# Row sums with the residual's addition, squares on ScalarE, rows normalised a chunk later

## What is computed

```python
x = layernorm(x + attn(x))      # attn: time-mixed k, v, r; WKV scan; gate; product with Wo
x = layernorm(x + ffn(x))       # ffn: 8 experts, the 2 best per token, 256 -> 1024 -> 256

def layernorm(x, eps=1e-5):
    m = mean(x, -1); v = var(x, -1)
    return (x - m) / sqrt(v + eps)

# the scan, per channel d and batch b, over the 2048 tokens
no  = max(o, u + k);  y = (exp(o-no)*p + exp(u+k-no)*v) / (exp(o-no)*q + exp(u+k-no))
no2 = max(w + o, k);  p, q, o = exp(w+o-no2)*p + exp(k-no2)*v, exp(w+o-no2)*q + exp(k-no2), no2
attn = (sigmoid(r) * y) @ Wo.T
```

## Time and profile before

| | |
|---|---|
| median of 3 runs | 699.39 us (697.89 to 700.32) |
| the profiled execution's own time | 698.79 us |
| its span in the profile | 696.8 us |
| busy: PE, DVE, ACT, POOL | 630.9, 464.1, 377.9, 333.2 us |
| chain that ended last, by engine | PE 64%, DVE 16%, issue 8%, ACT 4%, DMA 3%, POOL 2% |
| DVE busy in slices 4 to 13 of 40 (52 to 226 us) | 9 or more tenths up to slice 12 |

### The profile page before, as it was taken

One profiled execution on the slowest core, in us unless ns is written; L12 is line 12 of the kernel. 1 busy time (PEld: TensorE's weight loads), 2 busy tenths in 40 slices (PEclk: granted clock), 3 DMA queues, 4 the chain that ended last, 5 costly groups with the idle time before them and its releaser, 6 DMA issues.

```text
span 696.8 us, 14651 instructions
## 1 busy us (share of the span) xinstructions
PE 630.9 (91%) x4525; PEld 581.3 (83%) x4525; DVE 464.1 (67%) x1075; ACT 377.9 (54%) x690; POOL 333.2 (48%) x322
## 2 busy tenths in 40 slices
PE   8999999999977788999999999999999999999800
PEld 5787887878854578999999999999999999999700
DVE  4879999999998566556556565565565465545334
ACT  3566686585764133645464646466464646464317
POOL 6111037536546768239356384356394275222325
PEclk9999999999989779999999999999999999999955
DMA  8500222321324745532534425325317313231376
GB/s 254 157 32 0 91 91 70 132 83 55 107 86 154 232 148 151 162 60 63 144 48 146 71 42 160 60 49 144 72 24 183 47 42 47 48 48 15 36 226 276
DMA packets 53309, 70.61 MB, mean 101 GB/s; under 512 B 5482, under 2 KB 46900, under 8 KB 53076
## 3 DMA queue, kind: packets, MB, share of 16 engines
q1 hardware_dynamic: 31012, 43.24, 18.8%
q0 software_dynamic: 13216, 17.09, 13.4%
q10 hardware_dynamic: 8976, 8.82, 4.5%
HBM read 40.86 MB, written 29.06 MB: 100 GB/s over the span
## 4 chain that ended last, share of the span: by engine, by line
PE 64%; DVE 16%; issue 8%; ACT 4%; DMA 3%; POOL 2%; SPq 0%; DVEq 0%; ACTq 0%; POOLq 0%
PE hT_ps L871 27%; PE y_ps L880 26%; PE vr_ps L708 3%; PE k_ps L708 2%; PE xT_ps L889 2%; ACT zz L1133 2%; DVE o_all L1221 2%; POOL records_dram L614 2%; DMA zz<-x_dram 1%; DVE newton L1244 1%; DVE newton L1249 1%; DVE stats L1319 1%; DVE newton L1242 1%; DMA recs<-records_dram 1%; DVE num L1311 1%
## 5 line engine op out<-in xcount | busy, mean ns | idle before, releaser
L871 PE MATMUL hT_ps<-xTh,wx 128*128 128x256 f32 x1120 | 207.5, 283 | 2.6 <-DVE aTl L1191 1.3
L652 POOL DMA_INDIRECT x_dram<-y_sb,dest x70 | 108.5, 1550 | 195.3 <-DVE y_sb L1208 128.1
L880 PE MATMUL y_ps<-wx,aTh 128*128 128x256 f32 x1088 | 191.1, 279 | 3.0 <-DVE y_sb L1208 3.0
L871 PEld LDWEIGHTS hT_ps<-xTh,wx 128*128 128x128 f32 x1120 | 174.8, 189 | 3.3 <-DVE aTl L1191 2.4
L1191 DVE TENSOR_TENSOR aTl<-hT_ps,aTh 128x512 fp32r<-128x512 f32 x140 | 93.3, 688 | 121.7 <-ACT aTh L1094 121.7
L880 PEld LDWEIGHTS y_ps<-wx,aTh 128*128 128x128 f32 x1088 | 165.5, 189 | 3.4 <-issue 3.4
L871 PE MATMUL hT_ps<-xTl,wx 128*128 128x256 f32 x560 | 156.9, 280 | 0.0
L880 PE MATMUL y_ps<-wx,aTl 128*128 128x256 f32 x544 | 151.7, 279 | 0.0
L1088 ACT ACT_TABLE_LOAD x33 | 42.3, 1283 | 162.5 <-PE hT_ps L871 160.8
L1088 ACT ACTIVATE hT_ps<-hT_ps,b_c 128x256 f32<-128x256 f32 x280 | 113.5, 468 | 22.8 <-PE hT_ps L871 21.2
L614 POOL DMA_INDIRECT records_dram<-rec,slot_i x64 | 76.7, 1198 | 67.6 <-DVE rec L1352 35.9
(11 more groups left out here) (203 smaller groups left out, 853.5 us busy)
## 6 DMA issues: line engine op xcount, KB each, us to landing
staging<-in_L_ffn_W SPq DMA_DIRECT2D x16, 1024.0 KB
recs<-records_dram ACTq DMA_DIRECT2D x33, 261.0 KB, 3.0
xin<-in_L_attn_x SPq DMA_DIRECT2D x16, 256.0 KB, 4.3
xres<-in_L_attn_x SPq DMA_DIRECT2D x16, 256.0 KB, 3.1
x_dram<-rec SPq DMA_DIRECT2D x16, 256.0 KB, 3.4
zz<-x_dram SPq DMA_DIRECT2D x8, 512.0 KB, 9.2
out<-zz SPq DMA_DIRECT2D x8, 512.0 KB, 3.5
records_dram<-pad_rec SPq DMA_DIRECT2D x8, 261.0 KB, 2.9
```

The costliest lines, as they stand in the source:

```text
L652: pool.indirect_dma_start(sums, bass.IndirectOffsetOnAxis(ap=dest[t.slot][:, h:h + 1], axis=0), y_sb[t.slot][:, h, :], None, bounds_check= ...
L871: ins = pe.matmul(hT_ps[b][:, f, :], wx[:, s, part, off:off + P], xpart[t.slot % 2][:, cc, :], start=k == 0, stop=k == len(terms) - 1)
L880: ins = pe.matmul(y_ps[h], apart[t.slot % 2][:, fc, h * P:(h + 1) * P], wx[:, s, part, off:off + C], start=k == 0, stop=k == len(terms) - 1)
```

## The change

DVE: each of the two residual additions per chunk becomes two instructions of 128 x 256 (one per tile) that also write the sum of the row into `sum_1`. `statistics` is gone (four bn_stats, four bn_aggr). ACT: a new stage `square_rows` of chunk i-1 stands where `normalise_x1` stood: one ACTIVATE makes -mean of the four tiles from `sum_1`, then four ACTIVATEs square (row - mean) and write the sums into `sum_2`; each of these waits for the one before. `normalise_x1` now runs in step i on chunk i-2, between `exponents` and `bonuses`. POOL: `spread_of` waits for the squares, and has three operations in place of four. `sum_1` is one buffer: the first residual addition of a chunk waits until -mean of the chunk before is made (`mean_done`).

```diff
@@ POOL @@
             def spread_of(c):
-                pool.wait_ge(mv_done, c.upto(J))
-                pool.tensor_tensor(var_e[:], mv[:, :, 1], eps_b[:], ALU.add).then_inc(vare_done, 1)
-                pool.tensor_scalar(neg_mean[:], mv[:, :, 0], -1.0, 0.0, ALU.mult, ALU.add).then_inc(vare_done, 1)
-                pool.wait_ge(vare_done, c.upto(3, 2))
+                pool.wait_ge(squared, c.upto(J))
+                pool.tensor_scalar(var_e[:], sum_2[:], 1.0 / C, EPS, ALU.mult, ALU.add).then_inc(vare_done, 1)
+                pool.wait_ge(vare_done, c.upto(2, 1))
@@ ACT @@
+            def square_rows(c):
+
+                act.wait_ge(res_done, c.upto(RES))
+                after(act, rstd_done, (c - 1).upto(1))
+                act.activation(neg_mean[:], sum_1[:], ACT.Copy, scale=-1.0 / C).then_inc(mean_done, 1)
+                act.wait_ge(mean_done, c.upto(1))
+                for j in range(J):
+                    after(act, squared, c.number * J + j)
+                    act.activation(squares[:], xres[c.slot][:, j // TH, j % TH, :], ACT.Square, bias=neg_mean[:, j:j + 1],
+                                   accum_out=sum_2[:, j:j + 1]).then_inc(squared, 1)
@@ ACT, step @@
+                if (i - 2).exists:
+                    normalise_x1(i - 2)
+                if i.exists:
                     bonuses(i)
...
                 if (i - 1).exists:
-                    normalise_x1(i - 1)
+                    square_rows(i - 1)
@@ DVE @@
-            def statistics(c):
-                dve.wait_ge(res_done, c.upto(2))
-                for j in range(J):
-                    dve.bn_stats(stats[:, j, :], xres[c.slot][:, j // TH, j % TH, :]).then_inc(bn_done, 1)
-                dve.wait_ge(bn_done, c.upto(J))
-                take_wait(dve)
-                for j in range(J):
-                    dve.bn_aggr(mv[:, j, :], stats[:, j, :]).then_inc(mv_done, 1)
@@ DVE, add_residual @@
-                dve.tensor_tensor(xres[c.slot][:, b], wo_bank(c, b), xres[c.slot][:, b], ALU.add).then_inc(res_done, 1)
+                    after(dve, mean_done, (c - 1).upto(1))
+                for h in range(TH):
+                    dve.scalar_tensor_tensor(out=xres[c.slot][:, b, h], in0=wo_bank(c, b)[:, h, :], scalar=1.0, in1=xres[c.slot][:, b, h],
+                                             op0=ALU.mult, op1=ALU.add,
+                                             accum_out=sum_1[:, b * TH + h:b * TH + h + 1]).then_inc(res_done, 1)
```

More of the change, by code:

```diff
@@ L186, in build @@
         neg_mean = sb("neg_mean", [P, J])
-        stats = sb("stats", [P, J, 6])
-        mv = sb("mv", [P, J, 2])
+        sum_1 = sb("sum_1", [P, J])
+        sum_2 = sb("sum_2", [P, J])
+        squares = sb("squares", [P, C])
         phase_a = ExitStack()
@@ L295, in build @@
         ln_done, r0_done, div_done, mixed_done = sem("ln_done"), sem("r0_done"), sem("div_done"), sem("mixed_done")
-        wo_done, res_done, bn_done, mv_done = sem("wo_done"), sem("res_done"), sem("bn_done"), sem("mv_done")
+        wo_done, res_done, mean_done, squared = sem("wo_done"), sem("res_done"), sem("mean_done"), sem("squared")
         vare_done, rstd_done, x1_done = sem("vare_done"), sem("rstd_done"), sem("x1_done")
@@ L320, in build @@
         c_bn, c_mv, c_var, c_rstd, c_res = (sem(n) for n in ("c_bn", "c_mv", "c_var", "c_rstd", "c_res"))
+        RES = B * TH
         REC_DMAS = 2 * J * 16
@@ L586, in spread_of @@
             def spread_of(c):
-                pool.wait_ge(mv_done, c.upto(J))
-                pool.tensor_tensor(var_e[:], mv[:, :, 1], eps_b[:], ALU.add).then_inc(vare_done, 1)
-                pool.tensor_scalar(neg_mean[:], mv[:, :, 0], -1.0, 0.0, ALU.mult, ALU.add).then_inc(vare_done, 1)
-                pool.wait_ge(vare_done, c.upto(3, 2))
+                pool.wait_ge(squared, c.upto(J))
+                pool.tensor_scalar(var_e[:], sum_2[:], 1.0 / C, EPS, ALU.mult, ALU.add).then_inc(vare_done, 1)
+                pool.wait_ge(vare_done, c.upto(2, 1))
                 pool.tensor_tensor(rstd[:, c.slot, :], var_e[:], half_neg[:], ALU.pow).then_inc(vare_done, 1)
-                pool.wait_ge(vare_done, c.upto(3))
+                pool.wait_ge(vare_done, c.upto(2))
                 pool.tensor_tensor(shift[:, c.slot, :], neg_mean[:], rstd[:, c.slot, :], ALU.mult).then_inc(rstd_done, 1)
@@ L765, in project_out @@
                         pe.wait_ge(gate_in, 48)
-                    after(pe, res_done, (c - 1).upto(2))
+                    after(pe, res_done, (c - 1).upto(RES))
                 elif c.number >= NCH - 2:
@@ L769, in project_out @@
                 else:
-                    pe.wait_ge(res_done, c.upto(2, 1))
+                    pe.wait_ge(res_done, c.upto(RES, TH))
                 pe.wait_ge(mixed_done, c.upto(B, n + 1))
@@ L783, in turn_early @@
                 if n == 0:
-                    pe.wait_ge(res_done, Step(None, NCH - 1, 2, NCH).upto(2))
+                    pe.wait_ge(res_done, Step(None, NCH - 1, 2, NCH).upto(RES))
                 else:
@@ L1377, in step @@
                     stages = [(stabilise, i)] + opening + [(divide, i - 1), (place, i - 3), (accumulate, i), (residual_0, i - 1), (numerator, i),
-                              (residual_1, i - 1), (statistics, i - 1), (choose, i - 2), (lower_halves, i + 2)]
+                              (residual_1, i - 1), (choose, i - 2), (lower_halves, i + 2)]
                     if i.number == NCH - 1:
@@ L1381, in step @@
                 elif i.number == NCH:
-                    stages = [(divide, i - 1), (residual_0, i - 1), (residual_1, i - 1), (statistics, i - 1), (choose, i - 2),
+                    stages = [(divide, i - 1), (residual_0, i - 1), (residual_1, i - 1), (choose, i - 2),
                               (place, i - 2)]
```

## The result

The changed kernel takes 704.72 us (median of 5 runs, 703.1 to 706.71) where the kernel before takes 699.39 (697.89 to 700.85): ratio 1.0069, 95% interval 1.0044 to 1.0095. It is slower by 0.7%, 5.3 us. The profiled execution took 704.72, span 702.9. Times within a kernel are those of its one profiled execution; for whole kernels the ratios count.

What follows compares the result with a forecast made beforehand. The prediction took DVE to bound the full steps, PE's chain a floor 1.05 us below. Terms +0.4 (step 2), -0.7, -0.9, +3.4, +0.4 sum to +2.6 us: 701.4 by the profiled execution, 702.0 as median, range 696.5 to 706.5.

Steps and rivals of the forecast that it cites:

- S = 3.0 us: ACT's `square_rows` per chunk: -mean 0.2 plus four squares with their sums at 0.70 each; ends 2.2 and 3.6.
- Rival 1: Sums nearly free on ACT: squares 2.2 us (deciding below 2.35), steps at PE's floor 25.15, end +1.8; 696.3 us; chance 0.17.
- DVE's additions, +0.25 per batch row: DVE's residual additions: two instructions for one add 0.19 us, the sum perhaps 0.1; 0.25 per batch row, 0.5 per chunk.
- Rival 4: DVE's additions with a sum run at half rate, 0.27 us more per 256 columns; 703.6 us; chance 0.05.
- ACT bounds the steps at 25.95, three times -0.25: Three full middle steps: ACT's loop of 22.93 plus the squares replaces DVE's 26.20 us; -0.7 in all.
- DVE's work per step falls to 24.85 us, below PE's floor: Full steps: DVE's 26.20 us lose 1.85 of statistics and gain 0.5 of additions; PE's floor is 25.15.
- My part on POOL: POOL: one of four tiny operations goes, `spread_of` takes 1.6 us and hides in a middle step.
- Step 6, -0.9 and a start of step 7 1.2 us earlier: Step 6: DVE's own work counts, -1.85 + 0.5, with 0.5 of waiting for scores; step 7 begins 1.2 us earlier.
- End of the phase, +3.4: Last chunks, cover gone: odds, squares, `spread_of`, rows in a chain; last rows transposed at 241.4 for 237.95, +3.4 us.
- PE's clock, +0.4: End of the phase: longer PE idle ahead of 224.5 may keep the clock low through idle products; half of 0.8 us.
- Rival 3: End of the phase: something else already holds the last rows, leaving only the steps' gain, -1.2; 698.2 us; chance 0.1.
- rival 2: Squares dear at 3.6 us (deciding above 3.25): ACT's loop 26.55 bounds every step, end +5.4; 706.5 us; chance 0.2.

Runs made afterwards that it cites:

- e_bufs: Changed kernel with four result buffers for the squares, so no square waits for the one before; ratio 1.0036 to the kernel before.
- e_order: Changed kernel with ACT squaring the rows ahead of the odds in steps 7 and 8; ratio 1.001 to the kernel before.
- e_hold: Changed kernel with DVE's divide of chunk 7 waiting until POOL is through with `spread_of` of chunk 6; ratio 1.0056 to the kernel before.
- e_tail_old: Changed kernel with DVE's old statistics for chunks 6 and 7, squares on ACT for chunks 0 to 5; ratio 0.9955 to the kernel before.
- e_move: Kernel before with rows normalised one chunk later and nothing else, statistics still on DVE; ratio 1.0011 to the kernel before.
- e_mid_old: Changed kernel with chunks 0 to 5 as before, squares on ACT for chunks 6 and 7 alone; ratio 1.0057 to the kernel before.

## Why the prediction was right, and where it was not

The forecast was 702.0 in a range of 696.5 to 706.5, "slower" the likeliest side. The time was 704.7: the side and the place of the loss were right, the size was short by 2.7 us. The middle steps came out near the forecast in part by luck, since two errors in ACT's loop cancel. By its steps:

- **S = 3.0 us**: 2.63. The square and its sum are as priced (0.51 and 0.19), but the read of the sum begins 0.1 us before the square ends, and the wait costs 0.14. Rival 1's bound of 2.35 was not reached; e_bufs, with 2.20, crosses it and still has 1.0036: the stretched operations keep DVE busy without a gap, 25.8 to 26.2 us a step, so the time before step 7 fell by 1.1 us and not by 4.9, and its end takes 5.4 us more than before where the rival had 1.8.
- **DVE's additions, +0.25 per batch row**: about +0.1 (a pair takes 0.67 us until the next operation, 107.16 to 107.83; the one addition of 512 columns took 0.58, 106.10 to 106.68 in the trace of before). Rival 4 is out: 411 ns for 256 columns, no half rate. The Trainium skill, "Vector Engine (DVE) Microarchitecture Reference", section "Points that are easy to get wrong", names the half rate for two SBUF sources only; the prediction took it to spare a source in PSUM, and the 411 ns agree.
- **"ACT bounds the steps at 25.95, three times -0.25"**: half right. ACT's loop in the changed kernel is 26.06 us (141.28 to 167.34): 4.41 to the end of the inverse, S 2.63, 0.95, 0.10, 3.79, 2.12 to PE's start on the rows, and 12.06 back to the copy of x. S is 0.37 below the forecast and the way back 0.50 above (11.56), so the sum fits by luck. PE's idle ahead of the rows was 0.2 to 0.3 us, not 0.5 to 1. The three steps gained nothing in this trace: 78.96 us for 78.59, with the dip in it. The same steps took 78.16 in e_order, 78.03 in e_hold and 77.39 in e_tail_old, so the 0.7 forecast lies inside what executions show.
- **"DVE's work per step falls to 24.85 us, below PE's floor"**: this step failed. It is about 25.85 in the changed kernel (26.05 less 0.20 idle), and in e_tail_old DVE is the bound at 25.8 with no idle: 24.85 less 0.3 (cheaper additions) plus 1.35 of stretched operations is 25.9. My part on POOL took its operations at their bare length, asked whether they hide and never what they hit. I counted the three operations of `spread_of` and left out that POOL's piece of the weights stands behind them in the queue and moves with them.
- **Step 6, -0.9 and a start of step 7 1.2 us earlier**: `b2v` of step 7 started at 205.02, 0.8 later than before. The steps gave 0.1 by `nd` (197.14 against 197.27); the piece that hits `newton` at 199.69 took 0.94 back.
- **End of the phase, +3.4**: with all before it, +7.5. Of the 4.9 us beyond the forecast (240.6 with the clock's 0.4), 2.0 are step 7's start, 2.2 are `spread_of` at 3.8 for 1.6, -0.7 is the cheaper S twice, 0.5 the transposes and idle products after 226.93 (3.5 us for 2.6, of which 0.4 was taken), 0.6 the scores (6.5 from the start of the out-projection for 5.9); 0.3 is unaccounted. The mechanism, cover gone and the odds ahead of the squares, is shown by e_order. The 2.2 us of `spread_of` are no part of it: they are POOL's collision again, which the prediction had nowhere.
- **PE's clock, +0.4**: of the right sign. The granted clock is 0.73 in 225 to 240 us against 0.78. In the next 15 us it is 0.61 in the changed kernel, 0.54 in the kernel before and 0.82 in e_move, which has the same last rows as before. The scores of chunk 7 took 3.58 us before and 1.95 in e_move, and the second phase's first product starts at 249.97 and 247.48. So between executions this clock is worth some 2.5 us, and no single span is evidence of less.
- Rival 3 ("the end hides it") is refuted by e_tail_old and e_mid_old, rival 2 by S.
- Two slips in the sums change nothing: `choose` of chunk 5, 1.35 us earlier, is 216.3 and not 216.2, and rival 1 gives 696.3 where the range starts at 696.5.

The 7.5 us at the last rows are 6.1 in the spans of the same two executions and 5.3 in the medians. Executions differ by 2 to 3 us in that clock and the second phase's; I didn't separate it further. ACT's first copy of x, which adds the 0.50 us to ACT's loop, starts 0.3 to 0.5 us late in the middle steps of some executions (idle 3.42 ahead of it at 141.28; 2.97 in the kernel before), with nothing in the profile to say why: this stays open.

## What to carry over

When an operation is moved on POOL or DVE, look up what the other engine runs at its new time, and what is queued behind it there: DVE operations with both sources in SBUF and POOL operations that read SBUF stretched each other here by about 1 us, and bare durations of either engine do not tell it. In this kernel, work that leaves a bound engine for a chain on another was best left where it was at the end of the pipeline, where no other chunk covers the chain (e_tail_old), or put ahead of whatever there waits for a third engine (e_order). And where the next floor is only 4% below a bound, expect less than the difference: here PE's dips of the clock, 1 us in each step that had one, had been hiding under DVE, and ACT's loop lay within 0.3 us of DVE's.

## What the runs showed of the hardware that I had not expected

POOL and DVE keep each other out. `var_e` (0.19 us alone) took 1.21 and ended with the DVE operation beside it; the power took 2.03 for 1.04; `spread` on DVE took 1.19 for 0.23 beside POOL's subtraction; of two that meet, either may be the one that waits. Even a small cast of DVE was held: `idxf`, 0.17 us on average before, took 0.44 at 141.37 and ended at 141.81, with the record DMA that POOL had begun to issue at 140.84. The Trainium skill, "SBUF — State Buffer", section "Who interferes with whom", has the rule: the two share one pair of ports, a DVE operation with two SBUF sources and a POOL operation that reads SBUF take it exclusively, and the second to issue waits. These traces agree for the operations with two sources, with the numbers above (the cast has one, and no run here isolates it), and this is the rule that the prediction should have weighed. By it the power of chunk 6 would start where `newton` ends, at 223.38, and end at 224.42, and it ended at 224.28.

An accumulated sum is an instruction of its own on both engines: 187 ns on ACT, 80 on DVE, both partly beside the operation they belong to.
